# A graph-attention and expert kernel: filing row numbers later, sums and relu placed elsewhere, fewer unread products

## The reference

```
x = x + gnn0(layernorm(x), adj)        # scores leaky_relu(src_i + dst_j), masked by adj, softmax, times h
x = x + ffn0(layernorm(x))             # top 2 of 8 experts, own layernorm, gelu, 512 hidden
x = x + relu-ed gnn1(layernorm(x), adj)
x = x + ffn1(layernorm(x))             # top 2 of 8 experts, gelu, 256 hidden
```

## Time and profile before

| | before |
|---|---|
| median of 3 runs | 971.91 us (971.05 to 973.93) |
| the profiled execution | 971.66 us, of which its span is 969.8 us |
| busy share of the span | PE 74%, VectorE 75%, GpSimd 56%, ScalarE 51% |
| chain of waits, by engine | PE 33%, VectorE 30%, issue 18%, POOL 8%, DMA 4%, ScalarE 4% |
| granted TensorE clock | mean 0.86 of 2.4 GHz |
| layer 0: blocks, turn to the groups, groups | to 199, 199 to 269, 269 to 484 us |
| layer 1: inputs, blocks, turn to the groups, groups | 484 to 508, 508 to 703, 703 to 737, 737 to 935 us |
| last sums and output | 935 to 970 us |

### The profile page before, as it was taken

The page is one execution under the profiler, slowest core; times in us unless marked ns, Lnnn a source line. Parts: engine busy times, 40 slices in busy tenths (PEclk is TensorE's granted clock), DMA queues, the critical chain, the costliest instruction groups (busy, mean ns, idle before and its releaser), DMA issues.

```text
span 969.8 us, 24555 instructions
## 1 busy us (share of the span) xinstructions
PE 721.8 (74%) x6577; PEld 572.6 (59%) x6632; DVE 724.3 (75%) x2663; ACT 490.7 (51%) x1113; POOL 546.4 (56%) x544
## 2 busy tenths in 40 slices
PE   3888787450899999999997888898358877877500
PEld 2666565350389999999845667776225665655400
DVE  6788887614179999999847999997544878787628
ACT  2556656310077777777605666656304655555335
POOL 0037777773037776776710077777773777777720
PEclk9977978755899999999999887778669999999855
DMA  8383344221123332232643444432242333333668
GB/s 220 120 167 105 104 120 94 75 69 49 45 52 91 91 87 83 82 87 80 178 141 101 122 148 145 145 94 70 74 115 73 106 103 98 93 106 95 210 238 323
DMA packets 129399, 111.47 MB, mean 115 GB/s; under 512 B 30306, under 2 KB 112681, under 8 KB 129352
## 3 DMA queue, kind: packets, MB, share of 16 engines
q1 hardware_dynamic: 112072, 77.04, 28.9%
q0 software_dynamic: 17280, 33.87, 10.8%
HBM read 60.32 MB, written 52.36 MB: 116 GB/s over the span
## 4 chain that ended last, share of the span: by engine, by line
PE 33%; DVE 30%; issue 18%; POOL 8%; DMA 4%; ACT 4%; SPq 1%; POOLq 1%; DVEq 0%; ACTq 0%
PE bank L632 9%; PE bank L646 9%; POOL y_buf L465 5%; PE bank L569 5%; DVE stat L913 4%; DVE xin L974 4%; PE bank L520 3%; POOL row_buf L457 3%; DMA y_buf<-g_y,g_dst 2%; DVE x1w L1008 2%; PE bank L517 2%; PE bank L618 2%; DVE x1w L1012 2%; PE bank L501 1%; DMA yin<-y_buf 1%
## 5 line engine op out<-in xcount | busy, mean ns | idle before, releaser
L465 POOL DMA_INDIRECT y_buf<-g_y,g_dst x284 | 294.2, 1036 | 167.5 <-issue 91.3
L457 POOL DMA_INDIRECT row_buf<-pay,slot x256 | 252.0, 985 | 216.4 <-DVE slot L1078 139.1
L807 ACT ACTIVATE g_xT<-bank 128x512 f16<-128x512 f16 x142 | 84.6, 597 | 206.2 <-PE bank L618 203.5
L632 PE MATMUL bank<-g_xT,w 128*128 128x256 f16 x1278 | 164.6, 274 | 1.9 <-ACT g_xT L807 1.8
L569 PE MATMUL bank<-cst,tri 128*128 128x512 bf16 x496 | 121.3, 389 | 54.7 <-issue 52.1
L632 PEld LDWEIGHTS bank<-g_xT,w 128*128 x1278 | 116.7, 98 | 19.2 <-issue 2.8
L569 PEld LDWEIGHTS bank<-cst,tri 128*128 128x128 bf16 x550 | 55.4, 101 | 114.4 <-issue 57.4
L646 PE MATMUL bank<-w,g_h 128*128 x1260 | 84.9, 220 | 16.3 <-DVE g_y L1229 16.1
L814 ACT ACTIVATE xn<-bank,b_cols 128x256 f32<-128x256 f32 x216 | 86.6, 473 | 19.0 <-PE bank L632 12.3
L814 ACT ACTIVATE xt<-bank,b_cols 128x256 f32<-128x256 f32 x210 | 84.2, 475 | 14.0 <-PE bank L632 10.9
L646 PEld LDWEIGHTS bank<-w,g_h 128*128 128x128 f16 x1260 | 76.4, 98 | 24.8 <-issue 22.5
(11 more groups left out here) (191 smaller groups left out, 1331.8 us busy)
## 6 DMA issues: line engine op xcount, KB each, us to landing
g_in<-row_buf SPq DMA_DIRECT2D x142, 130.0 KB, 2.3
yin<-y_buf SPq DMA_DIRECT2D x20, 512.0 KB, 4.9
x_buf<-x1w SPq DMA_DIRECT2D x16, 520.0 KB, 5.7
xin<-x_buf SPq DMA_DIRECT2D x10, 520.0 KB, 4.6
y_buf<-g_y,g_dst POOLq DMA_INDIRECT x284
xin<-in_x_dram SPq DMA_DIRECT2D x8, 512.0 KB, 5.0
adj_in<-in_adj_dram SPq DMA_DIRECT2D x16, 256.0 KB, 3.5
row_buf<-pay,slot POOLq DMA_INDIRECT x256, 2.4
```

The costliest lines, as they stand in the source:

```text
L457: pool.indirect_dma_start(row_buf[L][:, :], bass.IndirectOffsetOnAxis(ap=slot[q][:, k, t:t + 1], axis=0), pay[q][:, t, :], None).then_inc( ...
L465: pool.indirect_dma_start(y_buf[L][:, :], bass.IndirectOffsetOnAxis(ap=g_dst[k][:, t:t + 1], axis=0), g_y[k][:, t, :], None, bounds_check= ...
L632: last = nc.tensor.matmul(dst, w[:, bass.ds(e * (2 * HID[L]) + (wp * HID[L] + c * P), P)], g_xT[q][:, xp, :], start=(m == 0), stop=(m == 2))
L807: nc.scalar.activation(g_xT[q][:, :, :], x_ps[q], ACT.Copy).then_inc(s.gT_sb, 1)
```

## The change

In layer 0 the token numbers are filed when the groups are done, not ahead of the tables. The counts of unread products in layer 0's blocks go to zero (from 10 and 7), those ahead of the first group to 88 in layer 0 and 72 in layer 1 (from 96). In layer 1 the relu of the attention is written back to PSUM, the sums read it there, and PE waits for the sums in both layers, the first block included. The second expert result is added in a function of its own, `add_second`, called where `take_in` added it; only for the first two blocks is the order another: the sums of block 1 stand ahead of the scores of block 0.

```
-IDLE_EXP, IDLE_ATT = [10, 0], [7, 8]
-IDLE_START, IDLE_LOOP, IDLE_ST1, IDLE_GROUPS = 112, 8, 8, 96
+IDLE_EXP, IDLE_ATT = [0, 0], [0, 8]
+IDLE_START, IDLE_LOOP, IDLE_ST1, IDLE_GROUPS = 112, 8, 8, [88, 72]
...
-                    if L == 0 or not first:
-                        pe.wait_ge(SL[L].x_done if L == 0 else SL[L].rinv_ready, n + 1)
+                    pe.wait_ge(SL[L].x_done, n + 1)
...
-                with pe.Fori(0, IDLE_GROUPS // IDLE_LOOP):
+                with pe.Fori(0, IDLE_GROUPS[L] // IDLE_LOOP):
...
-                            last_copy = nc.scalar.activation(h_new[:, t:t + m, :], att[:, :, 0:D], ACT.Relu)
+                            last_copy = nc.scalar.activation(att[:, :, 0:D], att[:, :, 0:D], ACT.Relu)
...
-            def take_in(L, n, q, turn):
-
-                s = SL[L]
+            def add_second(L, n, q, turn):
+
                 if L == 1:
                     ch.wait()
                     ch.did(add_result(q, 1))
-                    ch.wait()
+
+            def take_in(L, n, q, turn):
+
+                ch.wait()
                 V.tensor_scalar(keep[:, :], adj_in[q][:, :, :].rearrange("p t j -> p (t j)"), 0.0, BIG,
-                                ALU.not_equal if L == 0 else ALU.is_gt, ALU.mult).then_inc(s.taken, 1)
+                                ALU.not_equal if L == 0 else ALU.is_gt, ALU.mult).then_inc(SL[L].taken, 1)
...
-                        last = V.scalar_tensor_tensor(x1w[q][:, t, X_AT:X_END], h_new[:, t, :], rinv[:, t:t + 1],
+                        last = V.scalar_tensor_tensor(x1w[q][:, t, X_AT:X_END], att_tile[1][t][:, 0:D], rinv[:, t:t + 1],
...
+                    if not (first or last or over):
+                        add_second(L, *block_at(i, d + 1))
                     if not (last or over):
                         take_in(L, *block_at(i, d + 1))
...
                 arrive(L, 0, 0, 0)
+                add_second(L, 0, 0, 0)
                 take_in(L, 0, 0, 0)
                 statistics_of(0, 0, True, iter(()))
                 split_second(L)
+                arrive(L, 1, 1, 0)
+                add_second(L, 1, 1, 0)
                 scores(L, 0)
-                arrive(L, 1, 1, 0)
                 step(0, 0)
...
                 if L == 0:
                     V.memset(h_sb[:, :, H_END:H_END + 1], 1.0)
+                group_tables(L)
+                split_first(L)
+                groups(L)
+                if L == 0:
                     for q in range(2):
                         dve.wait_ge(SL[0].scattered[q], 16 * TOP * TILES * NBLK // 2)
                     ch.did(file_under(cst[:, C_TOK:C_TOK + TILES]))
-                group_tables(L)
-                split_first(L)
-                groups(L)
```

## The result

The changed kernel takes 943.5 us (median of four runs, 941.78 to 946.23) against 971.48 us, a ratio of 0.9714 with a 95% interval of 0.9679 to 0.9749. The prediction's sum was 954.9, with a range of 943 to 968. The sign was right and the time is inside the range, but at its very edge: it lies where the rival "the clock holds in the first layer" had put it (940.5 to 944.5), so the term for layer 0's unread products has to be looked at. The profiled execution took 941.78 us, 29.9 less than the one before.

A forecast was written before the change was run, and what follows sets the result against it. No single engine was taken to bound the kernel; ahead of layer 0's first group scatter, tables, split and products ran one behind the other. Sum: 971.7 - 17.7 (first group earlier) - 3.1 (72 products) + 4.0 (layer 1's wait) = 954.9 us, range 943 to 968.

The forecast's parts named there:

- the clock holds in the first layer: Rival, chance 0.16: layer 0's steps stay near 20.8 us without unread products, total 940.5 to 944.5.
- the term for layer 0's unread products: Layer 0's blocks: without them steps run at the low clock, 22.7 us against 20.8; first group 10.4 us later.
- Filing: End of layer 0's blocks: tables and split no longer wait for the scatter; 28.1 us won if blocks stay unchanged.
- VectorE's wait for the older scatter: Last step of layer 0: this 4.31 us wait swallows 4.3 us of table 6's 14.7 us delay.
- Scatter beside the split: Layer 0's last table: POOL's scatter beside VectorE's split loses nothing, bounds 0 and 8.7 us.
- The 72 products: Ahead of layer 1's first group: 24 fewer products are 5.2 us, of which 3.1 are won before the rows decide.
- The wait for the sums: Layer 1's blocks: PE held until the sums are done costs 0.8 us a step, 4.0 over five steps.
- Second block's sums under the first one's scores: Start of layer 1: sums fill VectorE's 3.74 us idle time; nothing either way, bounds -0.8 and 0.7 us.
- Relu in PSUM: Layer 1's attention: eight sums take 2.23 us from PSUM against 2.19 from SBUF, so nothing.

The follow-up runs named there:

- products back: Changed kernel with 10 and 7 unread products a step put back in layer 0's blocks: 940.80 us, ratio 0.9673 to the kernel before.
- filing alone: Kernel before with only the filing of the token numbers moved behind the groups, 96 unread products kept: 944.10 us, ratio 0.9702.
- the two with products back and 72: Changed kernel with 10 and 7 products a step in layer 0, 72 ahead of its first group: 934.75 us; also with layer 1's relu and wait undone: 934.92 us.
- no products before: Kernel before with only the unread products of layer 0's blocks taken out: 977.23 us, ratio 1.0050.
- 72 alone: Changed kernel with 72 in place of 88 unread products ahead of layer 0's first group: 940.98 us, ratio 0.9678 to the kernel before.
- layer 1's wait undone: Changed kernel with layer 1's relu written to SBUF again and PE waiting for the reciprocals alone: 940.47 us, ratio 0.9681 to the kernel before.

## Why the prediction was right and wrong

**Filing: right.** Alone it gave 27.5 us with 96 products, where the term was 28.1 with 88. The working held within 1.2 us at each step: split 219.64 against 218.6 (the 0.9 of table 7 included), PE 1.0 behind it where 1.56 stood, 88 products in 22.0 against 20.8. The first product came at 242.49 where 241.0 stood for unchanged blocks.

**The unread products of layer 0: the mechanism was right, the size was three times too large, and this is the step that failed.** Means over the five profiles with 10 and 7 products (the kernel before, products back, filing alone, and the two with products back and 72) and the five with none (the changed kernel twice, no products before, 72 alone, layer 1's wait undone), in us:

| | with | without | difference | predicted |
|---|---|---|---|---|
| table 0 written | 59.95 | 61.94 | 2.0 | 3.3 |
| table 6 written | 182.78 | 188.19 | 5.4 | 14.7 |
| table 7 written | 197.28 | 200.50 | 3.2 | 10.4 |
| last scatter DMA issued | 229.20 | 233.43 | 4.2 | 14.7 |
| mean step, tables 0 to 6 | 20.5 | 21.0 | 0.6 | 1.9 |

The prediction put every step at the price of a slow one (22.7) against a mean of 20.8. One slow and one fast step of the changed kernel on PE, against the earlier trace rows:

```profile
80.02 0.23 PE L546 MATMUL bank<-hot_any,tri 128*128 128x64 bf16 x1 [2.88 <-DVE x1w L1009]
...
88.18 4.15 PE L524 MATMUL bank<-w_feat,xnT 128*128 128x144 f32 x16
94.81 1.97 PE L501 MATMUL bank<-cst,pair_e 128*128 128x128 f32 x8 [2.48 <-ACT pair_e L731]
96.62 3.84 PE L537 MATMUL bank<-h_sb,pair_eT 128*128 128x137 f32 x16
...
103.33 0.20 PE L546 MATMUL bank<-hot_any,tri 128*128 128x64 bf16 x1 [2.87 <-DVE x1w L1009]
...
107.84 0.65 PE L517 MATMUL bank<-xnT,to_score 128*64 128x256 f32 x4
109.37 2.18 PE L524 MATMUL bank<-w_feat,xnT 128*128 128x144 f32 x16
...
123.18 0.20 PE L546 MATMUL bank<-hot_any,tri 128*128 128x64 bf16 x1 [4.53 <-DVE x1w L1009]
```

Windows of these two steps, PE alone (columns as in the earlier trace rows):

```profile
80.00:92.00 12.00, 11.98 (x64) 0.50 0.46 132
103.00:112.00 9.00, 8.22 (x64) 0.81 0.66 162
```

In the first step the granted clock is 0.50 from transposes to features and attention takes 3.84, where the prediction's bound was 3.73: 23.3 us. In the second it rises between the two halves of the score products (their second half takes 0.65 where 1.12 is the slow value), and the step takes 19.85, though it too began slow. Over the five profiles without products 14 of 30 steps had slow features (3.8 us or more in place of 2.18) and took 21.6 to 23.4 us, and 16 took 18.6 to 20.3; with products 16 of 30 had them and took 20.9 to 22.0. So the products don't make slow steps rarer; they shorten a slow one by about 1 us (means 22.5 and 21.4) and the others by 0.4 (19.8 and 19.4). In these steps the exponentials' transposes and the attention run at full clock with products (attention 2.11 to 2.14 in every step of the five profiles) and mostly don't without (up to 3.85). Nor did PE idle the 5.0 us ahead of the ranks that the prediction added up: 29 of the 30 steps without products began behind 2.9 to 4.6 us. The row of one slow step was taken for the new kernel's every step, and the old mean for a kernel without slow ones. The remark that a long stretch of features may lift the clock "in some steps" was worth half of all steps. The rival "the clock holds" got the time right but not the reason: slow steps stand in every profile. That the after profile lost only 0.9 at table 7 is chance of both sides: the one of before was 1.8 behind its mean there, the one after 0.5 ahead of its own. What decides whether the clock rises before the features or behind them, no run here shows.

**VectorE's wait for the older scatter** absorbed its 4.3 as forecast in the run without products; in the means it absorbed 2.2 (5.4 at table 6, 3.2 at table 7), since the scatter itself came later.

**Scatter beside the split: the term was 0, bounds 0 and 8.7; measured 1.3.** From the first to the last DMA of table 7 POOL takes 20.6 and 20.5 us where the split comes later (kernel before, and before without products), and 21.4 to 22.6, mean 21.8, in the ten profiles where the split runs beside it. The Trainium skill's GPSIMD Engine Reference, section Specifications, warned of contention between GpSimd and VectorE instructions with two SBUF inputs, which the split's second half has; the traces agree on the sign at most, with a seventh of the price of a full hold-up. What causes the 1.3 is not shown: 0.8 of it lies in one pause between the first and second DMA, and SyncE's eight pad stores moved into the same stretch with the tables (in the kernel before they began at 237.16, behind the scatter):

```profile
206.66 8.89 SPq L379 DMA_DIRECT2D row_buf<-pad_row  x8
```

No run separates them from the split. In the changed kernel the 1.3 is hidden, as the rows have 4.1 us to spare; where PE waits for the rows, as in the profile of 72 alone, it is not.

**Layer 1.** The 72 products gave the forecast 3.1. The wait for the sums was forecast at 4.0 over five steps, and the five steps from the second sums to the seventh took 112.3 to 112.7 us in six profiles with the old wait and 113.9 to 115.4 in six with the new one: 1.9 on average. Over all seven steps the two groups overlap (155.1 to 158.1 and 156.1 to 161.2), and in the total no run resolves it. The term's bounds held, its path too (idle time, then features at 3.73 us, then a VectorE wait of 0.81 and 0.84 at L960, in two steps of the changed kernel's profile). Second block's sums under the first one's scores: forecast nothing; from input to first sums 27.43 became 26.88, VectorE going straight on to the scores:

```profile
471.58 4.41 DVE L973 SCALAR_TENSOR_TENSOR xin<-yin,xin 128x128 f32<-128x128 f32 x16 [12.83 <-DMA yin<-y_buf]
...
483.56 4.41 DVE L973 SCALAR_TENSOR_TENSOR xin<-yin,xin 128x128 f32<-128x128 f32 x16
487.88 0.68 DVE L960 SCALAR_TENSOR_TENSOR e_msk<-keep,bank 128x512 f32<-128x512 f32 x1
```

Relu in PSUM: eight sums 2.16 against 2.19, nothing.

With 3.2 for 10.4 and 1.9 for 4.0 the prediction's sum gives 945.6; the rest to 943.5 lies within the spread of single runs.

## What to carry to other kernels

A cost that comes and goes by itself, such as the clock in short steps, is priced from many steps or several profiles, not from one step against a mean: count how many of the steps before already pay it. When a wait at the end of a stage goes, look at once at what is ready second there. Here the rows had 4 us to spare, so 16 unread products fewer ahead of the first group, with those in the blocks put back to keep the scatter early, gave a kernel of 934.75 us, 7 to 9 below the changed one's two medians (941.55 and 943.5).

## What the runs showed of the hardware

POOL pauses once in each layer's last table. Between its first and second scatter DMA it idles longer than the usual 0.30 us, in each of the twelve profiles. In layer 0 the pause is 1.93 and 1.89 us in the two where the split comes later and 2.19 to 3.58 beside it. In layer 1, where split and scatter always run side by side, it is 1.83 to 2.63. No wait that the profiles show explains it, and its cause stays open.

The 64 bias products, of one column each, took 13.79 us in each of the twelve profiles, 0.215 a piece, whatever the layer's steps had been (granted clock 0.50 in them, before and after the change). Each loads its own weights, and in the kernel before PEld was busy 13.7 us with that.
